# Gathers that each wait for the one two places ahead, and an MLP sum that stands in front of the sixth product

## The chip, the cores and the metric

The kernel runs on one core of a Trainium2 chip. [...] Each engine takes its instructions in the order in which they are written, and engines wait for one another by semaphores. The metric is the device time of one execution in microseconds, the median of several.

## The reference

A batch of 2 sequences of 1024 tokens, width 128, goes through four layers, each added to its own input after a layer norm:

```
x = x + mixer_a(layernorm(x), ...)     # selective scan, 256 channels x 16 states
x = x + ffn(layernorm(x), ...)         # shared expert + top 2 of 8 experts, inner width 938
x = x + mixer_b(layernorm(x), ...)     # scan over 4 heads, then an MLP:
    h = silu(h @ gate_w.T) * (h @ up_w.T) @ down_w.T ; return res + h
x = x + ffn(layernorm(x), ...)         # the same weights
```

The kernel runs the expert layer twice, with the prefixes f (in front of mixer B) and g (behind it).

## The kernel before, in words

The token axis is cut into four chunks of 512 columns (`NCH` = 4).

**Expert layer** (`ffn_stage`). The router sorts the 4096 pairs of token and expert into 39 tiles of 128 rows (`SLOT_TILES`), by expert, 4 or 5 tiles to an expert. GpSimd gathers the token rows of tile j from memory by an indirect DMA into its own place `rows[:, j, :]` (L1067). Eight semaphores `x_loaded` serve the gathers in turn (`GATHERS` = 8), and `gathered(j)` is the count that says that gather j has landed. TensorE's `tile(j)` turns the rows (`turn_row`, L1229), does the down product of tile j-2 (L1214, L1217), turns the products of tile j-1 (L1196) and multiplies tile j with its expert's gate and up weights (`expert_half`, L1243 to L1245). The weights of an expert lie in one of three places of a ring. SyncE loads them raw (`load_expert`, L986 to L988) when the expert three places ahead has been used. GpSimd splits them into a high and a low half in four parts (`split_part`: L1047, L1049, L1052, L1055), the last of which signals `w_ready`. These parts stand between the gathers by a table: `BEHIND_GATHER` puts all four parts of expert 5 behind gather 33, for example, and those of experts 7 and 8 behind stores (L1078), the indirect DMAs that write a tile's result rows back. So a split waits for every gather in front of it. Gathers 0 to 3 go without a wait, and from 4 on they go in pairs: `GROUPS` holds 0, 4, 6, 8, ..., and at each of its members GpSimd waits for all gathers of the group in front.

**MLP of mixer B** (`mixer_b_stage`). It has 12 products (`NQ`), q = 0 to 11, three (`MT`) to a chunk. For each, TensorE does `gate_up(q)`: the gate product, then the up product (which waits for `low(q-3)`), each of three matmuls L2122 to L2124. ScalarE takes the silu of the gate (L2404), VectorE multiplies by the up product (L2658, "product q"), ScalarE writes the high half (L2317) and VectorE the low half (`low(q)`, L2621), and TensorE's `down(q)` adds the result to the chunk's sum. `finish(c)` on VectorE (L2627) adds the sum of chunk c to x; it waits for the third down product of the chunk and for GpSimd's `fold(c)` (L2457). TensorE's `centre_next(0)` (L2138), a matmul for the next layer's norm, waits for `finish(0)`. It stands behind `gate_up(6)`, `down(1)`, `down(2)` and `down(3)`, and in front of `gate_up(7)`.

Of the kernel before, what the change touches and what calls it, by code (L numbers as in the profile page):

```python
# [41 lines left out]
SLOT_TILES = (TOP * T + EXPERTS * (P - 1)) // P  # L42
# [34 lines left out]
def cols(c):  # L77
    return slice(c * CH, (c + 1) * CH)
# [760 lines left out]
def ffn_stage(k, d, which, tag, cleared, ready, out=None, logs=None, following=None):  # L839
# [53 lines left out]
    def gathered(j):  # L893
        before = len(range(j % GATHERS, SLOT_TILES, GATHERS))
        return 16 * (j // GATHERS + 1 + which * before)
# [80 lines left out]
    def down_of(ring, place):  # L976
        return ring[:, place, 2 * GW:EW].rearrange("p (i h m) -> p i h m", i=TILES, h=2)

    with stage, nc.Block(no_gpsimd_drain=True) as block:  # L979
# [52 lines left out]
        @block.gpsimd  # L1032
        def _(pool):
            PARTS, STORES = 4, 2
            GROUPS = [0] + list(range(4, SLOT_TILES, 2))
            BEHIND_GATHER = {3: [(2, 0), (2, 1), (2, 2), (2, 3)], 5: [(3, 0)], 7: [(3, 1)], 9: [(3, 2)], 11: [(3, 3)],
                             17: [(4, 0)], 19: [(4, 1)], 21: [(4, 2)], 23: [(4, 3)],
                             33: [(5, 0), (5, 1), (5, 2), (5, 3)], 35: [(6, 0), (6, 1)], 37: [(6, 2)], 38: [(6, 3)]}
            BEHIND_STORE = {1: [(7, 0)], 3: [(7, 1), (7, 2), (7, 3)], 7: [(8, 0)], 9: [(8, 1)], 11: [(8, 2)], 13: [(8, 3)]}

            def split_part(n, part):
                place = (n - 1) % RING
                high, low, dn = ring[:, place, 0:GW], ring[:, place, GW:2 * GW], down_of(ring, place)
                raw, raw_dn = raw_ring[:, place, GW:2 * GW], down_of(raw_ring, place)
                if part == 0:
                    pool.wait_ge(w_loaded[place], 48 * ((n - 1) // RING + 1))
                    nc.gpsimd.tensor_copy(high, raw).then_inc(w_high, 1)  # L1047
                if part == 1:
                    nc.gpsimd.tensor_copy(dn[:, :, 0, :], raw_dn[:, :, 1, :]).then_inc(w_high, 1)  # L1049
                if part == 2:  # L1050
                    pool.wait_ge(w_high, 2 * n - 1)
                    nc.gpsimd.tensor_tensor(low, raw, high.bitcast(F32), ALU.subtract)  # L1052
                if part == 3:
                    pool.wait_ge(w_high, 2 * n)
                    nc.gpsimd.tensor_tensor(dn[:, :, 1, :], raw_dn[:, :, 1, :], dn[:, :, 0, :].bitcast(F32),  # L1055
                                            ALU.subtract).then_inc(w_ready, 1)

            for part in range(PARTS):
                split_part(1, part)
            pool.wait_ge(k.first_row, 16)  # L1060
            pool.wait_ge(rows_stored, 16 * TOP * NCH)
            pool.wait_ge(source_ready, 1)
            for j in range(SLOT_TILES):
                if j and j in GROUPS:
                    for i in range(GROUPS[GROUPS.index(j) - 1], j):
                        pool.wait_ge(x_loaded[i % GATHERS], gathered(i))
                nc.gpsimd.indirect_dma_start(rows[:, j, :], None, k.xn_rows,  # L1067
                                             bass.IndirectOffsetOnAxis(ap=source[:, j:j + 1], axis=0))\
                    .then_inc(x_loaded[j % GATHERS], 16)
                for n, part in BEHIND_GATHER.get(j, []):  # L1070
                    split_part(n, part)

            pool.wait_ge(share_ready, 1)
            for j in range(SLOT_TILES):
                pool.wait_ge(outs_ready, j + 1)
                if j and j % STORES == 0:
                    pool.wait_ge(sent, sent_before + 16 * j)
                nc.gpsimd.indirect_dma_start(k.token_rows, bass.IndirectOffsetOnAxis(ap=back[:, j:j + 1], axis=0),  # L1078
                                             rows[:, j, :], None).then_inc(sent, 16)
                for n, part in BEHIND_STORE.get(j, []):  # L1080
                    split_part(n, part)
            for g in range(NCH):
                pool.wait_ge(out_loaded[g], 16 * TOP)
                part = slice(4 * g, 4 * g + 4)
                nc.gpsimd.tensor_tensor(both[:, 0, part, :], both[:, 0, part, :], both[:, 1, part, :], ALU.add)\
                    .then_inc(both_ready, 1)
            if following is not None:
                pool.wait_ge(next_loaded, 64)
                nc.gpsimd.tensor_scalar(following.w_in[:, :], following.w_in[:, :], k.vec[:, VB_NORM:VB_NORM + 1],
                                        (1.0 + 1e-6) ** -0.5, ALU.mult, ALU.mult).then_inc(following.weighed, 1)  # L1090
                pool.wait_ge(following.weighed, 1)
                a = DI + following.TAPPED * P
                nc.gpsimd.tensor_tensor(following.w_tap[:, :, :], following.w_tap[:, :, :],
                                        following.w_in[:, a:a + P].unsqueeze(1).to_broadcast([P, TAPS, P]), ALU.mult)\
                    .then_inc(following.weighed, 1)
# [774 lines left out]
def mixer_b_stage(k, d, spent, logs, given):  # L1870
# [6 lines left out]
    MT = 3  # L1877
# [101 lines left out]
    with stage, nc.Block() as block:  # L1979
# [543 lines left out]
        def _(dve):  # L2523
# [95 lines left out]
            def low(q):  # L2619
                dve.wait_ge(high_ready, q + 1)  # L2620
                nc.vector.tensor_tensor(p_at(1, q), ps[:, U[q % 3], :], p_at(0, q).bitcast(F32), ALU.subtract)\  # L2621
                    .then_inc(low_ready, 1)

            def finish(c):
                dve.wait_ge(tile_summed, (c + 1) * MT)
                dve.wait_ge(x_folded, c + 1)
                nc.vector.tensor_tensor(k.x[:, cols(c)], k.x[:, cols(c)], ps[:, O + 1 - c % 2, :], ALU.add).then_inc(x_added, 1)  # L2627
# [27 lines left out]
            for q in range(NQ):  # L2655
                dve.wait_ge(gate_done, q + 1)
                dve.wait_ge(u_ready, q + 1)
                nc.vector.tensor_tensor(ps[:, U[q % 3], :], gate[:, q % 2, :], ps[:, U[q % 3], :], ALU.mult)\  # L2658
                    .then_inc(prod_done, 1)
                if q:  # L2660
                    low(q - 1)
                if q % MT == 2 and q > MT:
                    finish(q // MT - 1)
            low(NQ - 1)
            finish(NCH - 1)

# [85 lines left out]
```

## Time and profile before

| | |
|---|---|
| median of 3 runs | 1002.78 us (1001.38 to 1005.39) |
| profiled execution: time, span | 1002.86 us, 1001.00 us |
| TensorE busy | 953.4 us (95%) |
| VectorE, GpSimd, ScalarE busy | 725.1, 616.6, 569.8 us |
| granted TensorE clock, mean | 0.986 of full speed |

The span runs from the first to the last instruction. Expert layer f lies at about 275 to 565 us, mixer B up to 703 us (its MLP from about 665), expert layer g behind it. A wait in the profile is the idle time of an engine in front of an instruction, put down to the event that ended it.

### The profile page before, as it was taken

The page shows a single profiled execution, that of the slowest core. Times are in us where ns is not written, and L with a number is a line of the kernel's source. Part 1 is how long each engine was busy: PE and PEld are TensorE (multiplying, and loading weights), DVE is VectorE, ACT ScalarE, POOL GpSimd, SP SyncE. Part 2 cuts the span into 40 slices and gives each one's busy share as a digit, 9 for nine tenths or more (in the row PEclk, how much of TensorE's full clock was granted, in tenths as well). Part 3 has the DMA queues.
Part 4 walks back from the last instruction along what each step waited for, and adds up shares of the span by engine and source line. Part 5 has one row for each costly group of instructions (what it writes and reads, how often), then busy time and mean ns, then how long its engine had stood idle before and what let it go on. Part 6 is the DMA issues. An engine that isn't in the chain of part 4 may idle for free. (4 is left out here: it accounts for less than half of the span.)

```text
span 1001.0 us, 16162 instructions
## 1 busy us (share of the span) xinstructions
PE 953.4 (95%) x4711; PEld 676.2 (68%) x4711; DVE 725.1 (72%) x1192; ACT 569.8 (57%) x1046; POOL 616.6 (62%) x482
## 2 busy tenths in 40 slices
PE   7988999988999999999999999998999999999997
PEld 2323333332467799899998556666666999999996
DVE  3999998999588666566665797775597666566666
ACT  6764655655542555555554788787723555555553
POOL 1599897999531856686541397852305764967432
PEclk9999989998999999999999999999999999999999
DMA  5233223353341123232011300000702222421104
GB/s 158 67 77 80 77 82 71 90 118 86 112 123 55 33 84 89 75 82 81 28 33 42 112 1 1 2 1 1 225 0 71 79 68 64 123 74 31 33 24 132
DMA packets 69248, 69.71 MB, mean 70 GB/s; under 512 B 14952, under 2 KB 51568, under 8 KB 69168
## 3 DMA queue, kind: packets, MB, share of 16 engines
q1 hardware_dynamic: 64176, 58.44, 20.2%
q0 software_dynamic: 4992, 10.23, 3.7%
q8 instruction: 46, 0.75, 0.3%
q14 instruction: 34, 0.28, 0.1%
HBM read 58.00 MB, written 10.62 MB: 69 GB/s over the span
## 5 line engine op out<-in xcount | busy, mean ns | idle before, releaser
L810 POOL TENSOR_TENSOR a_hc<-a_h,a_c_sb 128x512 f32<-128x512 f32 x128 | 159.7, 1272 | 45.1 <-DVE a_h L711 45.0
L492 PE MATMUL ps<-a_hc,eye 128*128 128x512 f32 x256 | 134.5, 641 | 12.6 <-POOL a_hc L810 12.0
L629 ACT ACTIVATE ps<-a_delta,a_neg_a 128x512 f32<-128x512 f32 x128 | 87.1, 689 | 73.5 <-DVE a_h L711 70.6
L492 PEld LDWEIGHTS ps<-a_hc,eye 128*128 128x128 f32 x256 | 45.6, 195 | 80.3 <-POOL a_hc L810 43.8
L1067 POOL DMA_INDIRECT f_rows<-xn_rows,f_source x39 | 37.4, 958 | 70.1 <-DVE f_source L1700 35.5
L1067 POOL DMA_INDIRECT g_rows<-xn_rows,g_source x39 | 37.3, 956 | 69.1 <-DVE g_source L1700 38.1
L711 DVE TENSOR_TENSOR_SCAN a_h<-ps,a_state,a_b_u 128x512 f32<-128x512 f32 x64 | 79.0, 1278 | 1.0 <-ACT ps L629 0.8
L1214 PE MATMUL ps<-g_ring_rounded,g_q_hi_rounded 128*128 x312 | 77.1, 337 | 0.0
L1214 PE MATMUL ps<-f_ring_rounded,f_q_hi_rounded 128*128 x312 | 77.0, 337 | 0.0
L711 DVE TENSOR_TENSOR_SCAN a_h<-ps,a_b_u 128x512 f32<-128x512 f32 x64 | 75.2, 1212 | 1.9 <-ACT ps L629 1.7
L691 DVE TENSOR_TENSOR a_b_u<-a_du,ps 128x1024 f32<-128x1024 f32 x57 | 68.5, 1202 | 0.9 <-PE ps L479 0.8
L1078 POOL DMA_INDIRECT token_rows<-f_rows,f_back x39 | 38.0, 975 | 49.0 <-DMA token_rows<-f_rows,f_back 23.3
L1078 POOL DMA_INDIRECT token_rows<-g_rows,g_back x39 | 38.0, 975 | 44.2 <-DMA token_rows<-g_rows,g_back 19.2
L1243 PE MATMUL ps<-f_ring_rounded,f_work_rounded 128*128 x156 | 62.1, 398 | 3.0 <-POOL f_ring_rounded L1055 1.8
L1773 DVE TENSOR_TENSOR f_prods<-f_work,ps 128x470 f32<-128x470 f32 x78 | 50.3, 644 | 18.0 <-PE ps L1245 14.3
L1243 PE MATMUL ps<-g_ring_rounded,g_work_rounded 128*128 x156 | 62.0, 397 | 1.0 <-DVE g_work_rounded L1758 0.6
L1418 ACT ACTIVATE f_work<-ps 128x470 f32<-128x470 f32 x78 | 44.0, 565 | 32.8 <-PE ps L1245 30.7
L1418 ACT ACTIVATE g_work<-ps 128x470 f32<-128x470 f32 x78 | 44.0, 564 | 30.2 <-PE ps L1245 27.4
L1773 DVE TENSOR_TENSOR g_prods<-g_work,ps 128x470 f32<-128x470 f32 x78 | 50.3, 644 | 14.9 <-PE ps L1245 11.1
L1217 PE MATMUL ps<-f_ring_rounded,f_q_lo_rounded 128*128 x273 | 60.9, 223 | 0.0
L1217 PE MATMUL ps<-g_ring_rounded,g_q_lo_rounded 128*128 x273 | 60.9, 223 | 0.0
L1214 PEld LDWEIGHTS ps<-g_ring_rounded,g_q_hi_rounded 128*128 128x128 f32 x312 | 58.9, 189 | 2.8
(485 smaller groups left out, 2753.3 us busy)
## 6 DMA issues: line engine op xcount, KB each, us to landing
a_c_sb<-c_rows SPq DMA_DIRECT2D x64, 256.0 KB, 3.3
f_ring<-in_gu SPq DMA_DIRECT2D x16, 469.0 KB
g_ring<-in_gu SPq DMA_DIRECT2D x16, 469.0 KB
f_ring<-in_dn SPq DMA_DIRECT2D x8, 512.0 KB
g_ring<-in_dn SPq DMA_DIRECT2D x8, 512.0 KB
xn_rows<-f_work SPq DMA_DIRECT2D x8, 256.0 KB, 4.1
f_rows<-token_rows SPq DMA_DIRECT2D x8, 256.0 KB, 4.7
xn_rows<-g_work SPq DMA_DIRECT2D x8, 256.0 KB, 4.1
```

Source lines behind the costliest of these rows:

```text
L492: nc.tensor.matmul(ps[:, Y + f, :], k.eye[:, :], hc[:, s % WAITING, :], start=False, stop=(n == NST - 1)).then_inc(y_added, 1)
L629: nc.scalar.activation(ps[:, A + m % NA, :], delta[:, f, cols(g)], ACT.Exp, scale=neg_a[:, f, n:n + 1])\
L691: nc.vector.tensor_tensor(decayed_in[:, p:p + FT, :], du[:, :, cols(g)], ps[:, B + i % 2, :].unsqueeze(1).to_broadcast([P, FT, CH]), ALU.m ...
L711: nc.vector.tensor_tensor_scan(h[:, s % DEPTH, :], ps[:, A + m % NA, :], decayed_in[:, m % FEED, :], initial, ALU.mult, ALU.add).then_inc( ...
L810: nc.gpsimd.tensor_tensor(hc[:, m % WAITING, :], h[:, s % DEPTH, :], c_sb[:, i % RING, :], ALU.mult)\
L1067: nc.gpsimd.indirect_dma_start(rows[:, j, :], None, k.xn_rows, bass.IndirectOffsetOnAxis(ap=source[:, j:j + 1], axis=0))\
L1078: nc.gpsimd.indirect_dma_start(k.token_rows, bass.IndirectOffsetOnAxis(ap=back[:, j:j + 1], axis=0), rows[:, j, :], None).then_inc(sent, 16)
L1214: last = nc.tensor.matmul(ps[:, Y2, 0:2 * P], q_hi[:, j % 2, a], in_ring(place, w, w + 2 * P), start=(i == 0), stop=(i == NI), skip_group_ ...
L1217: nc.tensor.matmul(ps[:, Y2, 0:P], q_lo[:, j % 2, a], in_ring(place, w, w + P), start=False, stop=False, skip_group_check=True)
L1243: nc.tensor.matmul(out, xt[:, 0, j % 2, :], w_hi, start=True, stop=False)
L1418: nc.scalar.activation(gates[:, half, 0:HALVES[half]], ps[:, 2 * half, 0:HALVES[half]], ACT.Silu)\
L1773: nc.vector.tensor_tensor(prods[:, j % 2, half * H0:half * H0 + HALVES[half]], gates[:, half, 0:HALVES[half]], ps[:, 2 * half + 1, 0:HALVE ...
```

## The change

Two edits. From gather 4 on, each gather waits for the one two places ahead (gather 4 for 0 to 2) in place of pairs that wait for the whole pair in front. In the MLP the `finish` of the three first chunks stood behind the products 5, 8 and 11; the first now stands behind product 4, the others where they were.

```
-            GROUPS = [0] + list(range(4, SLOT_TILES, 2))
+            AT_FIRST, UNDER_WAY = 4, 2
...
             for j in range(SLOT_TILES):
-                if j and j in GROUPS:
-                    for i in range(GROUPS[GROUPS.index(j) - 1], j):
+                if j >= AT_FIRST:
+                    for i in range(0 if j == AT_FIRST else j - UNDER_WAY, j - UNDER_WAY + 1):
                         pool.wait_ge(x_loaded[i % GATHERS], gathered(i))
                 nc.gpsimd.indirect_dma_start(rows[:, j, :], None, k.xn_rows,
...
                 if q:
                     low(q - 1)
-                if q % MT == 2 and q > MT:
-                    finish(q // MT - 1)
+                if q in (4, 8, 11):
+                    finish((4, 8, 11).index(q))
             low(NQ - 1)
             finish(NCH - 1)
```

On GpSimd, in layer f before the change, these are gathers 28 to 33 and what follows them; `gathered4` stands for the semaphore that gathers 4, 12, 20, ... use:

```order
L1067 DMA f_rows<-xn_rows,f_source 128x128 [waits gathered3,gathered2]
L1067 DMA f_rows<-xn_rows,f_source 128x128
L1067 DMA f_rows<-xn_rows,f_source 128x128 [waits gathered5,gathered4]
L1067 DMA f_rows<-xn_rows,f_source 128x128
L1067 DMA f_rows<-xn_rows,f_source 128x128 [waits gathered7,gathered6]
L1067 DMA f_rows<-xn_rows,f_source 128x128
L1047 CAST f_ring_rounded<-f_ring 128x1876 [waits f_w_loaded1]
L1049 CAST f_ring_rounded<-f_ring 128x8x128
L1052 TENSOR_TENSOR f_ring_rounded<-f_ring,f_ring_rounded 128x1876 [waits f_w_high]
L1055 TENSOR_TENSOR f_ring_rounded<-f_ring,f_ring_rounded 128x8x128 [waits f_w_high]
```

The four last rows are the splits of expert 5. The same place after the change:

```order
L1067 DMA f_rows<-xn_rows,f_source 128x128 [waits gathered2]
L1067 DMA f_rows<-xn_rows,f_source 128x128 [waits gathered3]
L1067 DMA f_rows<-xn_rows,f_source 128x128 [waits gathered4]
L1067 DMA f_rows<-xn_rows,f_source 128x128 [waits gathered5]
L1067 DMA f_rows<-xn_rows,f_source 128x128 [waits gathered6]
L1067 DMA f_rows<-xn_rows,f_source 128x128 [waits gathered7]
L1047 CAST f_ring_rounded<-f_ring 128x1876 [waits f_w_loaded1]
```

No instruction has moved; the two waits of an even gather are shared out, one to each. On VectorE, in the MLP of mixer B, one instruction moves (L2658 is a product, here 4, 5 and 6, L2621 the low half of the product in front, L2627 `finish(0)`):

```order
 L2658 TENSOR_TENSOR ps<-b_gate,ps 128x512
 L2621 TENSOR_TENSOR b_bc_rounded<-ps,b_bc_rounded 128x512
+L2627 TENSOR_TENSOR x<-x,ps 128x512
 L2658 TENSOR_TENSOR ps<-b_gate,ps 128x512
 L2621 TENSOR_TENSOR b_bc_rounded<-ps,b_bc_rounded 128x512
-L2627 TENSOR_TENSOR x<-x,ps 128x512
 L2658 TENSOR_TENSOR ps<-b_gate,ps 128x512
 L2621 TENSOR_TENSOR b_bc_rounded<-ps,b_bc_rounded 128x512
```

`finish(0)` has gone ahead of product 5 and low(4). TensorE, ScalarE and SyncE keep their order.

## Rows read from the trace of the kernel before

**Rows 1.** The page, busy time of each engine
```profile
PE 953.4 (95%) x4711; PEld 676.2 (68%) x4711; DVE 725.1 (72%) x1192; ACT 569.8 (57%) x1046; POOL 616.6 (62%) x482
```
**Rows 2.** TensorE's waits, 400:440 and 675:720: us in total, times, longest
```profile
PE ps L1243 <- POOL f_ring_rounded L1055: 1.8, 1, 1.8
...
PE ps L2138 <- DVE x L2627: 2.2, 1, 2.2
```
**Rows 3.** Timeline of TensorE, expert 5 begins, in f and in g: start, us
```profile
419.80 1.03 PE L1196 MATMUL ps<-eye,f_prods 128*128 128x128 f32 x8
422.63 0.47 PE L1243 MATMUL ps<-f_ring_rounded,f_work_rounded 128*128 x1 [1.80 <-POOL f_ring_rounded L1055]
...
864.88 0.46 PE L1243 MATMUL ps<-g_ring_rounded,g_work_rounded 128*128 x1
```
**Rows 4.** Timeline of GpSimd, gathers and splits of f, last of g
```profile
364.09 0.95 POOL L1067 DMA_INDIRECT f_rows<-xn_rows,f_source  x1 [5.68 <-DMA f_rows<-xn_rows,f_source]
365.34 0.95 POOL L1067 DMA_INDIRECT f_rows<-xn_rows,f_source  x1 [0.30 <-issue]
368.51 0.95 POOL L1067 DMA_INDIRECT f_rows<-xn_rows,f_source  x1 [2.23 <-DMA f_rows<-xn_rows,f_source]
...
411.06 0.95 POOL L1067 DMA_INDIRECT f_rows<-xn_rows,f_source  x1 [2.45 <-DMA f_rows<-xn_rows,f_source]
...
413.25 1.78 POOL L1047 CAST f_ring_rounded<-f_ring 128x1876 fp32r<-128x1876 f32 x1
...
420.12 2.36 POOL L1055 TENSOR_TENSOR f_ring_rounded<-f_ring,f_ring_rounded 128x1024 fp32r<-128x1024 f32 x1
...
857.51 2.41 POOL L1055 TENSOR_TENSOR g_ring_rounded<-g_ring,g_ring_rounded 128x1024 fp32r<-128x1024 f32 x1
```
**Rows 5.** Line 1067: durations (ns), its waits, time from issue to landing
```profile
L1067 POOL DMA_INDIRECT f_rows<-xn_rows,f_source x39: 942/947/1172, 320.8 to 436.4; - x39
...
  DMA f_rows<-xn_rows,f_source: 26.2, 10
...
DMA to landing us min/median/max: 2.4/2.6/6.2
```
**Rows 6.** Timeline of SyncE: first issue for experts 5 and 7
```profile
377.73 0.33 SPq L986 DMA_DIRECT2D f_ring<-in_gu  x1
...
427.30 0.33 SPq L986 DMA_DIRECT2D f_ring<-in_gu  x1
```
**Rows 7.** Timeline of VectorE, the MLP: product 5, low(4), finish(0)
```profile
682.63 0.70 DVE L2658 TENSOR_TENSOR ps<-b_gate,ps 128x512 f32<-128x512 f32 x1 [3.64 <-ACT b_gate L2404]
683.23 0.69 DVE L2621 TENSOR_TENSOR b_bc_rounded<-ps,b_bc_rounded 128x512 fp32r<-128x512 f32 x1
683.84 0.68 DVE L2627 TENSOR_TENSOR x<-x,ps 128x512 f32<-128x512 f32 x1
```
**Rows 8.** Timeline of TensorE: last of down(2), of down(3), centre_next(0), gate_up(7)
```profile
681.40 0.40 PE L2124 MATMUL ps<-b_bc_rounded,b_w_lo_rounded 128*128 128x512 f32 x1
...
682.10 0.40 PE L2124 MATMUL ps<-b_bc_rounded,b_w_lo_rounded 128*128 128x512 f32 x1
684.66 1.10 PE L2138 MATMUL ps<-x,cent 128*128 128x512 f32 x2 [2.16 <-DVE x L2627]
685.19 0.80 PE L2122 MATMUL ps<-b_sz_rounded,b_w_hi 128*128 128x512 f32 x1
```
**Rows 9.** Timeline of ScalarE: the silus of products 5 and 6
```profile
682.00 0.60 ACT L2404 ACTIVATE b_gate<-ps 128x512 f32<-128x512 f32 x1
...
683.49 0.60 ACT L2404 ACTIVATE b_gate<-ps 128x512 f32<-128x512 f32 x1
```
**Rows 10.** Timeline of GpSimd, the folds of chunks 0 to 2
```profile
675.31 3.80 POOL L2457 TENSOR_TENSOR x<-x,xn 128x512 f32<-128x512 f32 x3
```
**Rows 11.** Windows: stretch, its us, busy us by engine, granted clock, DMA
```profile
125.00:150.00 25.00, 24.00 (x48) 8.92 (x48) 25.00 (x23) 14.47 (x22) 24.95 (x19) 0.88 0.28 82
...
311.00:550.00 239.00, 234.40 (x1530) 212.99 (x1529) 147.82 (x311) 121.93 (x254) 140.99 (x106) 1.00 0.21 62
```

## The prediction

> **What bounds the kernel now.** The busy table comes first: TensorE is busy for 953.4 of the 1001.0 us of the span, no other engine for more than 725.1 [rows 1]. An edit on GpSimd or VectorE is therefore worth what TensorE waits for it, and no more. So I read next the list of TensorE's waits in the two places that the diff touches. In the first expert layer (prefix f) it has one wait on GpSimd, 1.8 us, at the first weight product of a tile (L1243), for the low half of an expert's down weights (L1055). In the MLP of mixer B it has one of 2.2 us, at L2138, `centre_next(0)`, for the x that `finish(0)` adds up on VectorE (L2627) [rows 2]. The second expert layer (prefix g) shows no wait on GpSimd: the tile that begins a new expert there has its weights at 859.92 (857.51 + 2.41) and starts its first product at 864.88, so there are 4.96 us to spare [rows 3, 4].
>
> Third, the timelines, to see what each wait hangs on. In f TensorE's transposes end at 420.83 (419.80 + 1.03) and the product starts at 422.63 [rows 3]; the last split of expert 5 ends at 422.48 (420.12 + 2.36) [rows 4]. The four splits of expert 5 run back to back from 413.25; they stand behind gather 33 in GpSimd's order, and their raw weights were asked for at 377.73 [rows 6]. What made them late is the gathers: ten of them in f waited for an earlier gather's landing, 26.2 us in all, nine of the ten in front of 413.25 [rows 5].
>
> **Gathers, step by step.** An issue takes 0.95 us (median 947 ns) and the next follows 0.30 us later [rows 4, 5]. Before, gather j of an even number waits for both of the pair in front. Pair 14, 15 is issued at 364.09 and 365.34, the latter's issue ends at 366.29, and gather 16 starts at 368.51: 2.22 us from the end of an issue to the release, 4.42 us per pair [rows 4]. After, a gather waits for the one two places back. Gather 16 is then free at the end of 14's issue (365.04) + 2.22 = 367.26, 1.25 us sooner, and 17 is free 2.22 us after 15's issue, which is 1.25 us behind. A pair then costs 0.95 + 2.22 = 3.17 us in place of 4.42: 1.25 us saved (one issue and its gap) at each boundary at which GpSimd sat waiting. Nine such stand ahead of expert 5: 9 x 1.25 = 11.3 us. Bounds: nothing, if the landings follow one another at 2.2 us each whatever is in flight; at the top the waits themselves, all but 26.2 us [rows 5]. The two long ones (5.68 us before 364.09 is the longest) are landings beside an expert's weight load, and I keep them whole but for the 1.25. I take 11.3. The splits of expert 5 then end at about 411.2, and TensorE wants them at 420.83. Only 1.8 us of the 11.3 are needed, that is two of nine boundaries. **Term 1: -1.80 us**, all that the pause holds.
>
> The four issues at the start (j = 0 to 3) stay, and gather 4 is at no time held longer than before. Every gather has its own rows of `rows`, and no queue is passed: the same instructions stand in the same order on GpSimd. Stores and splits that come sooner are for later tiles; what lies behind gather 38 (the stores, with the splits of expert 7, whose load is issued at 427.30 [rows 6], 1.8 us sooner after) will reach expert 7's load some microseconds before it has landed and wait there, with stores queued behind that nobody waits for until the layer's end. The same gain of time in g lands on its 4.96 us of slack: 0.
>
> [...]
>
> **The MLP, step by step.** `finish(0)` needs the third down product, `down(2)`, whose last matmul starts at 681.40 and lasts 0.40: 681.80 [rows 8]. VectorE has nothing to do then: it waits 3.64 us, until 682.63, for ScalarE's silu of product 5 (q counts from 0; the "sixth product") [rows 7], which starts at 682.00 behind two table loads and ends at 682.60 [rows 9]. Before, `finish(0)` stands behind product 5 and low(4) and runs 683.84 to 684.52, and TensorE, which had issued its last `down(3)` matmul at 682.10, starts `centre_next(0)` at 684.66, 0.14 us behind it [rows 7, 8]. After, `finish(0)` runs 681.83 to 682.51, in VectorE's idle time. Its other condition, the fold on GpSimd, was met at 679.11 (675.31 + 3.80) [rows 10]. Product 5 starts at 682.63 as before, with 0.1 us to spare. `centre_next(0)` starts at 682.51 + 0.14 = 682.65, behind `down(3)`, which hands over at 682.33 to 682.50. **Term 2: 684.66 - 682.65 = -2.01 us.** Bounds: 0, and 2.16, the whole pause [rows 8].
>
> What is late next? `gate_up(7)` followed at 685.19, 0.53 us behind `centre_next(0)`; it goes to 683.18, and its up half, which needs low(4), to 684.28. Low(4) is not moved and ends at 683.92 (683.23 + 0.69) [rows 7]: 0.36 us to spare. Product 6 needs the silu that ends at 684.09 (683.49 + 0.60) [rows 9]. It then starts at 684.1, its low half follows, and all of it keeps ahead of a TensorE that has only moved by 2.01. `finish(1)` and `finish(2)` stand where they stood. Behind the pause TensorE runs without a break to the last of them, so the 2.01 us go through. The g layer's loads are issued from its own start and move along.
>
> **Sum.** The profiled execution took 1002.86 us (span 1001.00, 1.86 around it), 0.08 above the median of 1002.78. 1002.86 - 1.80 - 2.01 = 999.05; from the median 998.97. Forecast: 999.0 us, -0.38%.
>
> **Rivals.**
> - *Both pauses go (the forecast)*: 999.0. 0.75.
> - *The gathers gain nothing*: landings in series, or issues grown longer; the pause of 1.80 stays. Against it: the 2.22 us are release time rather than transfer, for the shortest landing is 2.4 us and the median 2.6 [rows 5]. 1002.78 - 2.01 = 1000.8. 0.08.
> - *The MLP gains nothing*: `finish(0)` is released later than 681.83, and takes the sixth product's place. Up to 0.45 us of lateness costs nothing (0.1 before product 5, 0.36 before the up half); from there each microsecond costs one, and the gain is gone at 2.5. For it: the spare time at product 5 is only 0.1 us. 1002.78 - 1.80 = 1001.0. 0.07.
> - *Slower: the granted clock falls.* With both pauses gone TensorE is denser. The clock was 0.88 in 125 to 150 us, where TensorE was busy 24.00 of 25 us; it was 1.00 in 311 to 550 with 234.40 of 239 [rows 11]. The second row speaks against, for it is nearly as dense as it can be and holds. Price: 25 us at 0.88 cost 3.0 us; the gain of 3.8 is gone from 32 us at 0.88 on, and 75 us more at that clock give 999.0 + 9 = 1008. 0.04. [...]
> - *More than the forecast*: the pause in f hangs on landings that vary (2.4 to 6.2 us [rows 5]), so in other executions of before it can be longer than 1.80. Two more landings beside a load, (6.2 - 2.6) us each, would make it 9.0 and the gain 11.0: 991.8 in the limit, some 996.5 with a third of the excess. 0.06.
>
> **How the numbers follow.** The three runs before lie between 1001.38 and 1005.39, so about 0.5% (5 us) is what can be told from no change. The forecast lies inside: 3.8 us of 5. Range: the two one-term cases give 1000.8 and 1001.0 and the median of three may lie 1.2 above; below, the forecast less the same and less part of the last case: 996.5 to 1002.2. It leaves out the clock case and the far end of the last. Faster by over 0.5%: a fifth of the forecast's 0.75 by the spread of the runs, the last case and a little of the others, 0.23. Slower by over 0.5%: the clock case and the spread of the one-term ones, 0.07. The rest, 0.70, is within.
>
> **What would show it.** (1) No wait of TensorE at L1243 on GpSimd's L1055 in f; the splits of expert 5 end near 411, at any rate before 420.8. (2) Gathers without a split between them start 1.6 us apart on average, where it was 2.2, with issues still at 947 ns. (3) `finish(0)` in VectorE's wait ahead of product 5, that product still right behind the silu; TensorE's wait at L2138 down from 2.16 to about 0.15. (4) From there to the end every stage as long as before. I am wrong if a wait of TensorE appears on VectorE's L2621 or L2658 behind `centre_next(0)`, if gathers land later the more are in flight, or if the clock falls below 1.00 in the expert layers.

## The result and the profile after

Before, 17 runs have a median of 1004.14 us (999.24 to 1008.54); after, 17 runs have 999.77 (996.62 to 1001.38). The ratio is 0.9959, with a 95% interval of 0.9942 to 0.9976: 0.4% faster. The profiled execution of the changed kernel took 999.77 us, span 997.5, where that of before took 1002.86 with a span of 1001.0.

The busy row of the changed kernel's page stands where [rows 1] stood. In all rows PE is TensorE, which does the matmuls, PEld its weight loads, DVE VectorE, ACT ScalarE, POOL GpSimd and SP SyncE, which issues DMAs; `ps` is PSUM, the memory that the matmuls write.

```profile
PE 952.9 (96%) x4711; PEld 676.6 (68%) x4711; DVE 723.2 (73%) x1192; ACT 570.0 (57%) x1046; POOL 616.1 (62%) x482
```

The work is the same, only waits have gone. The list of TensorE's waits, of layer f (275 to 565) and of the end of the MLP (676 to 705), answers to [rows 2]: us in total, times, longest.

```profile
PE ps L1243 <- issue: 1.1, 2, 0.6
...
PE ps L2138 <- DVE x L2627: 0.2, 1, 0.2
...
PE ps L2225 <- DVE x L2627: 0.5, 1, 0.5
```

The wait at L1243 on GpSimd is gone from f, and that at L2138 is down from 2.16 us to 0.17. The timeline of GpSimd after shows why the first went; it answers to [rows 4]: gathers 24 to 33, and the first and last split of expert 5.

```profile
383.00 0.95 POOL L1067 DMA_INDIRECT f_rows<-xn_rows,f_source  x1 [0.66 <-DMA f_rows<-xn_rows,f_source]
...
398.50 0.94 POOL L1067 DMA_INDIRECT f_rows<-xn_rows,f_source  x1 [0.65 <-DMA f_rows<-xn_rows,f_source]
399.44 1.78 POOL L1047 CAST f_ring_rounded<-f_ring 128x1876 fp32r<-128x1876 f32 x1
...
406.33 2.38 POOL L1055 TENSOR_TENSOR f_ring_rounded<-f_ring,f_ring_rounded 128x1024 fp32r<-128x1024 f32 x1
```

Ten gathers start within 15.50 us, 1.72 us apart, where the same ten took 22.28, 2.48 apart; the splits end at 408.71 where it was 422.48. The view of L1067, against [rows 5]:

```profile
L1067 POOL DMA_INDIRECT f_rows<-xn_rows,f_source x39: 940/947/1172, 320.6 to 420.6; - x39
...
  DMA f_rows<-xn_rows,f_source: 11.8, 9
...
DMA to landing us min/median/max: 2.4/2.8/7.2
```

GpSimd waits 11.8 us for landings in f, where it was 26.2. In the MLP, VectorE and TensorE after, against [rows 7] and [rows 8]:

```profile
679.64 0.69 DVE L2627 TENSOR_TENSOR x<-x,ps 128x512 f32<-128x512 f32 x1 [2.84 <-PE ps L2124]
680.44 0.70 DVE L2658 TENSOR_TENSOR ps<-b_gate,ps 128x512 f32<-128x512 f32 x1
...
680.48 1.10 PE L2138 MATMUL ps<-x,cent 128*128 128x512 f32 x2 [0.17 <-DVE x L2627]
681.01 0.79 PE L2122 MATMUL ps<-b_sz_rounded,b_w_hi 128*128 128x512 f32 x1
```

`finish(0)` lies in VectorE's idle time, and product 5 (L2658) follows 0.11 us behind it, where its silu releases it.

Stage by stage: f, from its L1700 to the first L1307 behind it, took 236.0 us before and takes 234.0. The MLP, from its first silu (L2404) to L2138, took 13.8 and takes 11.8. Layer g, from its L1700 to its last L1307, takes 238.2 in both. So TensorE is 4.2 us earlier at L2138 (680.48 against 684.66), but the span is only 3.5 shorter. The difference arises at the border between mixer B and g and just behind it, as the timeline of TensorE there and the windows (us, busy by engine, granted clock, DMA share, GB/s) show. Of the changed kernel:

```profile
699.38 1.10 PE L1100 MATMUL ps<-x,cent 128*128 128x512 f32 x2 [1.05 <-PEq L1979]
700.76 1.19 PE L1112 MATMUL ps<-w_gate,xn 128*128 128x8 f32 x8 [0.29 <-DVE xn L1516]
701.81 3.52 PE L1105 MATMUL ps<-g_q_hi,ones 128*128 128x512 f32 x4
...
702.00:704.00 2.00, 2.00 (x3) 0.96 (x4) 0.23 (x1) 0.10 (x1) 0.00 (x0) 0.50 1.10 367
```

And of the kernel before, at the same place:

```profile
705.87 1.96 PE L1105 MATMUL ps<-g_q_hi,ones 128*128 128x512 f32 x4
...
706.00:708.00 2.00, 2.00 (x8) 0.99 (x8) 0.43 (x1) 1.14 (x3) 0.00 (x0) 1.00 1.11 359
```

The clock fell to 0.50, the lowest value of any window of 1 us in the fourteen profiles, behind two short idle times of 1.05 and 0.29 us and eight small matmuls; four matmuls took 3.52 us in place of 1.96. The same idle times in the kernel before left the clock at 1.00. From L1100 to the shared expert's first product (L1126) TensorE now takes 6.14 us where it took 4.46, so 1.7 us are lost. From there to layer g's L1700 it takes 49.9 us where it took 50.9, so 1.0 of them came back in this pair of profiles.

### The profile page after: what moved, and what is told of

Same layout as the page of the kernel before. It is cut to its first block and busy times, and to the rows that moved or that the text cites. A ratio compares the mean times of both kernels' runs of the same rounds, so it can differ in the third digit from the quotient of the medians.

```text
span 997.5 us, 16126 instructions
## 1 busy us (share of the span) xinstructions
PE 952.9 (96%) x4711; PEld 676.6 (68%) x4711; DVE 723.2 (73%) x1192; ACT 570.0 (57%) x1046; POOL 616.1 (62%) x482
## 5 line engine op out<-in xcount | busy, mean ns | idle before, releaser
L1214 PE MATMUL ps<-g_ring_rounded,g_q_hi_rounded 128*128 x312 | 77.1, 337 | 0.0
L1214 PE MATMUL ps<-f_ring_rounded,f_q_hi_rounded 128*128 x312 | 77.0, 337 | 0.0
L1067 POOL DMA_INDIRECT g_rows<-xn_rows,g_source x39 | 37.2, 954 | 58.8 <-DVE g_source L1700 38.1
L1067 POOL DMA_INDIRECT f_rows<-xn_rows,f_source x39 | 37.3, 957 | 54.6 <-DVE f_source L1700 35.5
L1078 POOL DMA_INDIRECT token_rows<-f_rows,f_back x39 | 37.9, 972 | 49.6 <-DVE f_rows L1752 26.9
L1243 PE MATMUL ps<-f_ring_rounded,f_work_rounded 128*128 x156 | 62.1, 398 | 1.1 <-issue 1.1
L1243 PE MATMUL ps<-g_ring_rounded,g_work_rounded 128*128 x156 | 62.0, 398 | 1.0 <-DVE g_work_rounded L1758 0.6
L1214 PEld LDWEIGHTS ps<-g_ring_rounded,g_q_hi_rounded 128*128 128x128 f32 x312 | 58.9, 189 | 2.8
```

The source lines that it names most:

```text
L1214: last = nc.tensor.matmul(ps[:, Y2, 0:2 * P], q_hi[:, j % 2, a], in_ring(place, w, w + 2 * P), start=(i == 0), stop=(i == NI), skip_group_ ...
L1243: nc.tensor.matmul(out, xt[:, 0, j % 2, :], w_hi, start=True, stop=False)
```

## The experiments

They were made on three chips; the runs of before beside them have medians of 1003.75, 1003.97 and 1002.77 us. "Faster" and "slower" below rest on the intervals of the ratios. The first four separate the two parts and give the pause in f two doses, one each way.

**The gathers alone** (the MLP as before):

```diff
-                 if q in (4, 8, 11):
-                    finish((4, 8, 11).index(q))
+                if q % MT == 2 and q > MT:
+                    finish(q // MT - 1)
```

> The gather edit alone, the MLP as before. Theory (each edit takes away one pause of TensorE): the 1.8 us pause at L1243 in layer f is gone, the splits of expert 5 end near 408.7 us as with both edits, the 2.16 us pause at L2138 stays; ratio about 0.998 (-1.8 to -2.5 us). Rival A (gather pace pays more than the pause in one profile shows, because the pause varies from execution to execution): -3 us or more, ratio 0.997 or less, and its executions spread less than those of the kernel before. Rival B (the gathers gain nothing): 1.000.

Measured: 1001.55 us, 0.9978 (0.9958 to 0.9997). No wait on GpSimd at L1243, the wait at L2138 back to 2.2, f 234.0.

**The MLP alone** (the gathers in pairs, as before):

> The MLP edit alone, the gathers in pairs as before. Theory: pause at L2138 0.15 to 0.2 us in place of 2.16, pause at L1243 in f of about 1.8 us stays; ratio 0.998 (-2.0 us), perhaps 0.5 to 1.5 us less of it if the granted clock falls at the border of mixer B and layer g, as it did in the profile of the changed kernel. Rival A: only this edit pays, ratio 0.996. Rival B: the moved sum gives its gain back in the g layer, 1.000.

Measured: 1000.69 us, 0.9973 (0.9953 to 0.9994); the waits L1243 2.0, L2138 0.2, f 236.1. Each half gives its pause, and the two ratios multiply to 0.9951, near the 0.9959 of the whole.

**Pairs, splits of expert 5 earlier.** If lateness of the splits is all that the gathers cost, moving the splits must do as well as faster gathers:

```diff
-                             33: [(5, 0), (5, 1), (5, 2), (5, 3)], 35: [(6, 0), (6, 1)], 37: [(6, 2)], 38: [(6, 3)]}
+                             29: [(5, 0), (5, 1), (5, 2), (5, 3)], 35: [(6, 0), (6, 1)], 37: [(6, 2)], 38: [(6, 3)]}
```

> The kernel before, with the four splits of expert 5 behind gather 29 in place of gather 33; gathers still in pairs, MLP as before. Theory (the pause in f is nothing but a split that stands behind too many gathers): the splits of expert 5 end some 8.8 us sooner (four gathers at 2.2 us), near 413.7, the pause at L1243 is gone, and the time is that of the gather edit alone, ratio about 0.998. Rival (the two-ahead waits pay in another way, by more overlap in the DMA queues or a freer GpSimd): the pause goes, but the time stays above that of the gather edit alone by 1 us or more.

Measured: 1002.23 us, 0.9988 (0.9969 to 1.0007). The pause is gone and f takes 234.0, as expected; the total alone would not have told it from the kernel before, nor from the gathers alone (1001.55). Its mixer A, ahead of f and the same code in all, took some 3.5 us longer in the profile, and the MLP behind the pause at L2138 took 1.6 us longer, with the clock at 0.50 from 687 to 689 us; more of this below.

**Pairs, splits later**, the other dose:

```diff
-                             33: [(5, 0), (5, 1), (5, 2), (5, 3)], 35: [(6, 0), (6, 1)], 37: [(6, 2)], 38: [(6, 3)]}
+                             37: [(5, 0), (5, 1), (5, 2), (5, 3)], 38: [(6, 0), (6, 1), (6, 2), (6, 3)]}
```

> The kernel before, with the splits of expert 5 behind gather 37 in place of 33 and those of expert 6 behind gather 38; pairs, MLP as before. Theory: four gathers at 2.2 us more in front, so the splits end 8.8 us later; the pause in f grows from 1.8 to 10.6 us, and in g, where there were 5.0 us to spare, one of 3.9 us appears (up to 7 if the gathers there meet the load of expert 6). Time +12.7 us, up to +16; ratio 1.013 to 1.016. Rival (GpSimd is ahead anyway, the wait is not set by the gathers): under +3 us.

Measured: 1023.63 us, 1.0222 (1.0187 to 1.0258). The waits of TensorE, one in f and one in g:

```profile
PE ps L1243 <- POOL f_ring_rounded L1055: 12.0, 1, 12.0
...
PE ps L1243 <- POOL g_ring_rounded L1055: 6.9, 1, 6.9
```

Slower by 20.1 us of span, where 16 was the most expected: 12.0 us of wait in f where 10.6 were expected, 6.9 in g where 3.9 to 7 were. Less the 1.8 of before, the two waits are 17.1 of the 20.1. The rest goes with the granted clock, which fell to 0.50 during the wait of f and stood at 0.55 for the first 4.4 us behind it, and at 0.69 on average around the wait of g (878 to 889 us). It is the same wait at the same line, fed by the same instruction. With the early dose it shows the cause of the pause: the place in time of expert 5's splits.

**The changed gathers with the same late splits.** Do denser gathers cover a delay that pairs can't?

> The changed kernel with the same late place of the splits of expert 5 (behind gather 37, those of expert 6 behind 38). Theory: with two-ahead waits four gathers cost 1.6 us each, so the splits in f end 6.4 us later than the changed kernel's 408.7, at about 415, still in front of the 420.8 at which TensorE wants them: no pause in f; in g a pause of 0 to 2 us. Time 0 to +2 us against the changed kernel, ratio to the kernel before 0.996 to 0.999. Rival (the gathers' pace is not the cause): as large a pause as with the pairs, over 8 us.

Measured: 1008.73 us, 1.0052 (1.0023 to 1.008). TensorE waits for no split, in f or g (the last of expert 5 ends at 414.38), so the gathers gained what was put down to them. But f takes 241.7 and g 240.4, with waits that no edit explains: L1214 on `f_q_hi_rounded` 1.5, L1196 on `f_prods` up to 2.2. This was a miss, and the next run makes it large.

**Three ahead**: `AT_FIRST, UNDER_WAY = 4, 3`.

> The changed kernel with each gather waiting for the one three places ahead. Theory: the gathers run faster still (pace near the issue's 1.25 us where no weight load runs beside them), the splits of expert 5 end 3 to 6 us sooner than 408.7, and the time does not change, for TensorE no longer waits for them: ratio 0.996. Rival (faster gathers pay by themselves): 1 us or more below the changed kernel. Second rival (more in flight, later landings: the pace stays at 1.6 us).

Measured: 1022.88 us, 1.0187 (1.0162 to 1.0213), span 1020.5. GpSimd now waits for landings only three times in f, 4.6 us in all, and yet f takes 249.6 and g 245.0. TensorE's waits of f that are new:

```profile
PE ps L1214 <- issue: 6.0, 1, 6.0
PE ps L1214 <- DVE f_q_hi_rounded L1746: 2.8, 1, 2.8
```

They are 8.8 of the 15.6 us by which f is longer than in the profile of the changed kernel. Most of the rest goes with the granted clock, 0.66 in the stretch of 362 to 372 us and 0.57 in that of 390 to 402, where the kernel before has 1.00 in both. Now what stands ahead of the longest wait, first on TensorE, then on ScalarE, then on SyncE's queue:

```profile
384.16 0.34 PE L1214 MATMUL ps<-f_ring_rounded,f_q_hi_rounded 128*128 x1
...
387.77 0.28 PE L1229 MATMUL ps<-eye,f_rows 128*128 128x128 f32 x1
394.03 0.58 PE L1214 MATMUL ps<-f_ring_rounded,f_q_hi_rounded 128*128 x1 [5.99 <-issue]
...
386.66 0.37 ACT L1400 ACTIVATE f_work<-ps,f_share 128x128 f32<-128x128 f32 x1 [3.60 <-remote]
389.51 0.60 ACT L1395 ACTIVATE f_q_hi_rounded<-ps 128x512 fp32r<-128x512 f32 x1 [2.49 <-remote]
...
386.65 0.34 SPq L986 DMA_DIRECT2D f_ring<-in_gu  x1
```

The last down product of the tile ends at 384.50 (384.16 + 0.34). ScalarE, which waits for it (semaphore `summed`) and has nothing else to do, starts at 386.66; SyncE, which waits for the same semaphore, issues at 386.65. Two engines freed at one moment, 2.16 us behind the matmul, were waiting for one signal, and the signal was late: `remote` means here no other core, but a signal that the view can't put down to an instruction. In the eight profiles without a late signal, the kernel before among them, ScalarE's L1400 starts within 0.04 us of the end of a down product (L1214) in every tile of f and g. Two more come late behind it. The signals themselves, as the trace has them (us, semaphore number):

```
386.633 S217
389.492 S227
392.364 S227
392.415 S223
392.466 S224
392.517 S223
392.568 S224
392.602 S220
```

Six signals arrive within 0.24 us, for work on TensorE that takes about 2.6 us. The matmuls had been done and their signals had piled up; the steps between the late ones are 2.86 and 2.87 us. Meanwhile GpSimd issues gathers without any wait for a landing, seven in a row at 1.25 us from start to start:

```profile
384.70 0.94 POOL L1067 DMA_INDIRECT f_rows<-xn_rows,f_source  x1 [0.30 <-issue]
```

**MLP: the third sum behind product 10** in place of 11, on the changed kernel: `if q in (4, 8, 10)`.

> The changed kernel, with the sum of the third chunk one product sooner too (behind product 10 in place of 11). Theory: TensorE's wait of 0.5 us at L2225 (the third chunk's centring) goes, nothing else moves: -0.5 us against the changed kernel in the trace, not to be told in the time, ratio 0.9955. Rival: the sum now waits in front of product 11 for down(8) and delays it; TensorE then waits 0.3 to 0.7 us at the last down products, and nothing is gained.

Measured: 1004.93 us, 1.0002 (0.9984 to 1.002). The wait of 0.5 at L2225 is gone, and L2138 to L2225 takes 14.7 us where it takes 15.3, so the edit does what it says. The time doesn't show it: f takes 237.9, and the chip's runs of before are at 1003.97.

**MLP: the first sum between product 5 and its low half**, half of the old delay:

```diff
+                if q == 5:
+                    finish(0)
...
-                if q in (4, 8, 11):
-                    finish((4, 8, 11).index(q))
+                if q in (8, 11):
+                    finish((8, 11).index(q) + 1)
```

> The changed kernel, with the first chunk's sum behind the sixth product and in front of its predecessor's low half, in place of ahead of both. Theory: the sum starts 0.8 us after the silu-bound product and not before it: it ends near 683.8 on the old clock, and the pause at L2138 is 1.3 to 1.5 us (between 0.17 and 2.16); low(4) is 0.6 us later and costs nothing more. In the trace +1.3 us against the changed kernel at that place. Rival: low(4), now later, holds the up half of the next gate_up, and the pause moves to L2122.

Measured in one execution: 1007.37 us, span 1005.1. The wait at L2138 is 1.6 us, L2225 0.5, none at L2122. So the pause goes by the place of `finish(0)`: 2.2 behind the low half, 1.6 ahead of it, 0.2 ahead of the product. f takes 238.6, with a wait of 2.5 at L1214.

The last four runs ask, on a third chip, whether the late signals belong to the gathers, and what version does without them.

**The changed kernel again**, unchanged:

> The changed kernel itself once more, beside its parts on one chip. In four profiles of kernels with two-ahead or three-ahead gathers ScalarE began a tile's L1400 instruction 2 to 4 us behind the matmul that releases it, and TensorE then waited 2.4 us or more at L1214 in layer f; in the profile of the changed kernel it did not. Theory A (the two edits are worth 1.8 and 2.0 us, and the late releases belong to the chip or the execution): ratio 0.996 again, or on a chip that shows late releases about 0.999, with a wait at L1214 of 2 us or more in its profile. Theory B (the late releases come with the later place of the third sum or another edit of those kernels): 0.996 and no wait at L1214.

Measured: 1002.37 us (998.34 to 1009.88), 0.9996 (0.997 to 1.0022): no gain that the interval shows on this chip. Both pauses are gone as before, but f takes 236.2 and g 239.0. The late signal of f, on TensorE, ScalarE and TensorE again:

```profile
392.60 0.33 PE L1214 MATMUL ps<-f_ring_rounded,f_q_hi_rounded 128*128 x1
...
395.19 0.37 ACT L1400 ACTIVATE f_work<-ps,f_share 128x128 f32<-128x128 f32 x1 [2.64 <-remote]
...
398.34 0.38 PE L1214 MATMUL ps<-f_ring_rounded,f_q_hi_rounded 128*128 x1 [0.89 <-DVE f_q_hi_rounded L1746]
```

The matmul ends at 392.93 and ScalarE starts 2.26 us later. Ahead of it gathers start about every 1.4 us.

**The gathers alone again**:

> The gather edit alone once more, on the same chip as the others of this set. Theory A (late releases come from the denser gathers, on some chips): it gains the 1.8 to 2 us pause and loses what TensorE waits at L1214; ratio 0.998 without late releases, 1.000 to 1.003 with them. Theory B (they don't come from the gathers): 0.998 whatever the others show.

Measured: 1006.41 us, 1.0012 (0.9985 to 1.004). f 237.3, g 238.9, signals late by 2.88 and 1.02 us.

**Groups of three**: the pairs' way of waiting, `GROUPS = [0] + list(range(4, SLOT_TILES, 3))`, on the kernel before.

> The kernel before with gathers in groups of three from gather 4 on (each group waits for the whole group in front), MLP as before. It tells what makes the releases late. Theory A (gathers that never drain: two-ahead keeps one or two in flight at all times): groups of three drain each time, so no L1400 is late, the splits of expert 5 end about 5 us sooner than with pairs, the pause at L1243 is gone: ratio 0.998. Theory B (a burst of three issues 1.25 us apart is enough): L1400 is late by over 1 us in f or g, with a wait at L1214, ratio 1.000 or more.

Measured: 1002.09 us, 0.9999 (0.9971 to 1.0027). The splits of expert 5 end at 419.33, there is no wait on GpSimd, and no late signal, so a burst of three issues is not enough to bring one; f 235.3, g 238.9. It keeps the old MLP, whose wait at L2138 is 2.2.

**Pairs, with the MLP's edit and the early splits**: the table's 33 moved to 29, and `if q in (4, 8, 11)`.

> The MLP edit, the gathers in pairs as before, and the splits of expert 5 behind gather 29 in place of 33. Theory: it takes away both pauses (1.8 at L1243 in f, 2.0 at L2138) without denser gathers, so ratio 0.996 on every chip, no late release of L1400 and no wait at L1214. If the chip shows late releases with two-ahead gathers, it is 2 us or more faster than the changed kernel; if not, the same. Rival (the denser gathers pay for themselves somewhere else): slower than the changed kernel by over 1 us.

Measured: 999.31 us (998.1 to 999.95), 0.996 (0.9939 to 0.9981), on the chip where the changed kernel had 1002.37. No late signal, no wait on GpSimd; f 234.0, the last split:

```profile
409.99 2.40 POOL L1055 TENSOR_TENSOR f_ring_rounded<-f_ring,f_ring_rounded 128x1024 fp32r<-128x1024 f32 x1
```

It removes both pauses and leaves the gathers as they were. On this chip its slowest execution is faster than eleven of the twelve of the changed kernel, though the intervals of the two ratios still touch. It is the best version found.

## Why the prediction was right, and where it was not complete

**Term 2, the MLP: right to 0.02 us.** The pause fell from 2.16 to 0.17, `finish(0)` took VectorE's idle time, product 5 kept its place behind the silu, and the stage is 2.0 us shorter. The pause at L2138 was 0.2 in all six other profiles of kernels with `finish(0)` ahead of product 5, and 2.2 in all that lack the edit.

**Term 1, the pause in f: right in cause and size.** f is 2.0 us shorter, 1.80 of it the pause. Its steps came out roughly. The splits end at 408.71, not 411.2; gathers start 1.72 us apart, not 1.6; landings have a median of 2.8 us in both layers together, not 2.6, but in f alone it is 2.8 where it was 2.9, so no slowing by more in flight is shown. GpSimd's waits for landings fell by 14.4, not 11.3. None of it touches the time, for what lies beyond the first 1.8 us is slack. The prediction gives no price of a later split; the one expected for the late dose was too low in f, 10.6 against 12.0 us. That no pause is left in `ahead_split5_late`, with the same table, bounds from the other side what the dense gathers gain.

**The sum, 999.0 against 999.77 measured.** TensorE was 4.2 us earlier at L2138: 2.0 by f, 2.0 by the MLP, and 0.2 by a mixer A that no edit touches. Then 1.7 were lost at the border and 1.0 came back behind it, in a stretch (L1126 to g's L1700) that takes 49.6 to 51.3 us in the fourteen profiles, in no order by the edits. That leaves 3.5 of span and 3.1 of profiled time (1002.86 to 999.77), since the time outside the span is 2.3 us where it was 1.9. So the total is right in part by luck: a loss that the prediction did not have was made up by chance, and on the third chip the same kernel gained nothing.

The loss is the rival of the falling clock, at a place and in a size that it had not named: not tens of microseconds in the dense layers, but 1.7 us at the border behind the MLP. It is not chance in one trace. With the MLP's edit, in one of its forms, L1100 to L1126 takes 6.1 to 7.0 us in five profiles of eight, at a clock of 0.50 to 0.60, and 4.46 in the other three; in the six profiles without the edit it takes 4.46 each time. But two of these six, `pairs_split5_early` and `gathers_only_again`, have a dip of their own, right behind the pause that the edit closes. Of the latter, the end of the pause and then a window:

```profile
687.21 2.05 PE L2138 MATMUL ps<-x,cent 128*128 128x512 f32 x2 [2.16 <-DVE x L2627]
...
688.00:690.00 2.00, 2.00 (x5) 1.09 (x4) 0.26 (x1) 0.00 (x0) 0.72 (x1) 0.50 0.00 0
```

L2138 to L2225 takes 16.9 us in these two and 15.3 in the other four, and no profile with the edit has a dip there. So the old pause cost 1.6 us more than its own length in two executions of six, and the kernels with the edit pay about as much at the border in five of eight. Whether the edit brings a dip more often or only moves it, these profiles don't tell, and no run was made to test it. Two of the eight are the changed kernel itself, one with the dip and one without; `finish_between`, which kept a pause of 1.6 us, had it at the border. These dips stand behind idle times of TensorE; the rival argued from its density, and of that no run shows an effect. In the rival's own row, 0.88 for 25 us, 125 to 130.5 us stands at 0.50, with idle times of 1.60 us in front and 1.00 within, and 131 to 150 at 1.00, with TensorE busy for all of the 19 us. The changed kernel has 1.00 in 311 to 550 us, with TensorE busy for 236.08 of 239. Idle time is not all of it either: the kernel before has a dip at 581 us, behind 32 matmuls of 128x4, where TensorE was not idle for 10 us. No run here shows why the same pauses did no harm in other executions.

**"GpSimd's denser gathers cost nothing" was the step that failed**, though not in the profile by which the change was measured. The prediction let only GpSimd's own time and the landings speak against it. In six of the eight profiles with gathers two or three ahead, TensorE's signals came late and TensorE itself then waited at L1214 or L1196; in none of the six with pairs or groups of three. With two ahead it costs f 2.2 to 4.6 us (236.2, 237.3, 237.9 and 238.6 against 234.0), which is all of term 1 or more, and with the late splits beside it f took 241.7. In g these kernels take 238.8 to 239.0 against 238.2, but groups of three take 238.9 too, without a late signal, so I put nothing down to it there. (Their f, 235.3, is also 1.3 above 234.0, for a reason that I did not find.) This fits the 0.9959 and the 0.9996 that the same kernel has in two sets of runs. Chip and version are partly mixed: the changed kernel's own first profile had no late signal, nor had the one of dense gathers on the first chip; on the second chip all four had one, but no profile of pairs was taken there. Only the third has both, two late with dense gathers and two clean without.

**The other rivals.** "The gathers gain nothing" and "the MLP gains nothing" are excluded by the two runs of one part. The case of more than the forecast did not come up in f: the pause was 1.8 and 2.0 in the two profiles that have it undisturbed. Of the signs by which the prediction said it would be wrong, one did come up: the clock was below 1.00 in an expert layer, at the start of g, so that not every stage behind the MLP was as long as before. It cost 1.7 us, less than the room that the range had.

## What to carry to other kernels

Where a pause hangs on work that is late in an in-order queue, first try to move that work ahead by a few places: here it gave the same 2 us as faster transfers did, without more of them in flight. Read a gain of a few tenths of a per cent stage by stage and on more than one chip; the total hid here a stage that gained and another that lost. When an engine's idle time is put down to nothing, look at what else was freed at that moment: two engines released together (here ScalarE at 386.66 and SyncE at 386.65 us) point at a late signal and not at late work.

## What the hardware showed that I had not expected

- **TensorE's signals came up to 3.97 us late.** The delays of L1400 behind the end of the matmul, at most 0.04 us in the eight profiles without a late signal, were 2.16 us in `three_ahead` (f), 2.26 and 1.37 us in `after_again`, 2.88 and 1.02 in `gathers_only_again`, 3.97 and 0.94 in `finish_4_8_10`, 3.95 and 0.71 in `finish_between`, 3.77 and 1.56 in `ahead_split5_late` (f and g). Gathers at 1.25 us apart without a wait go with the worst of it (f +15.6 us, g +6.8). What holds the signals is not settled: with more gathers in flight both their issues and their landings are closer together (gathers 24 to 33 of f start 1.72 and land 1.87 us apart in the changed kernel, 2.32 and 2.21 in `mlp_only`), and no run separates the two, nor tells why one chip showed none. The pace alone doesn't sort the profiles: gathers 24 to 33 of f start 1.72 and 1.77 us apart in the two dense ones without a late signal, and 1.49 to 1.82 in the six with one. Matmul ends in a profile are modelled; the reading rests on the second waiter and on the six signals within 0.24 us, which don't depend on them.
- **The clock at a stage border differs between executions of one program**: four matmuls took 1.96 or 3.52 us with the same work and the same pauses ahead of them. Of `mlp_only`, which has it too, first a window and then the instruction:

```profile
703.47:705.47 2.00, 2.00 (x5) 0.94 (x5) 0.55 (x1) 0.61 (x2) 0.00 (x0) 0.60 1.08 358
...
703.47 3.37 PE L1105 MATMUL ps<-g_q_hi,ones 128*128 128x512 f32 x4
```

- **The same dips change a stage that no edit touches.** From f's first L1307 to the first silu of the MLP it takes 115.2 us in eleven profiles, 116.9 in `gathers_only_again` and `mlp_and_split5_early`, and 113.5 in `threes`. In `threes` the clock stays at 1.00 from 580 to 588 us; in the kernel before it is 0.68 and 0.89 in the two halves of that time, and in `gathers_only_again` 0.65 and 0.50.
- **Mixer A varies by 3.5 us.** Its end, f's L1700, stands at 318.8 to 320.3 us in most profiles and at 323.0 to 323.3 in three of fourteen, with no difference in the code. This is as large as the whole gain, and can be a part of why single runs of one kernel lie 4 us to either side; its cause is open.
